# Attention on one core: a group's two softmax-sum accumulators are folded into one by an adding DMA before TensorE sums over keys

## What is computed

```python
x = x + 0.5 * ffn(layernorm(x), ...)      # 64 experts, top 6, plus a shared one
x = x + attn(layernorm(x), ...)
x = x + 0.5 * ffn(layernorm(x), ...)

def attn(x, ...):                          # 16 query heads of 32, one key/value head
    scores = einsum('bhsd,btd->bhst', q, k) / sqrt(32)
    attn = softmax(scores, axis=-1)        # over t, 2048 keys
    out = einsum('bhst,btd->bhsd', attn, v)
    return out.reshape(b, s, 512) @ Wo + bo
```

## Time and profile before

| | |
|---|---|
| median of 3 runs | 3182.35 us (3176.6 to 3187.31) |
| profiled execution | 3182.29 us |
| its span, first to last instruction | 3180.6 us |
| TensorE busy | 2770.0 us (87%) |
| VectorE | 2046.3 us (64%) |
| ScalarE | 1522.7 us (48%) |
| GpSimd | 2218.7 us (70%) |
| mean granted TensorE clock | 0.934 of full speed |
| DMA moved | 575.78 MB |

### The profile page before, as it was taken

The page is one execution under the profiler, slowest core; times in us unless marked ns, Lnnn a source line. Parts: engine busy times, 40 slices in busy tenths (PEclk is TensorE's granted clock), DMA queues, the critical chain, the costliest instruction groups (busy, mean ns, idle before and its releaser), DMA issues. The chain is left out here.

```text
span 3180.6 us, 44938 instructions
## 1 busy us (share of the span) xinstructions
PE 2770.0 (87%) x15264; PEld 1651.1 (52%) x15264; DVE 2046.3 (64%) x3922; ACT 1522.7 (48%) x2871; POOL 2218.7 (70%) x1430
## 2 busy tenths in 40 slices
PE   7967777388899999999999999999999776888870
PEld 4644444166455555555555555555554464555540
DVE  7843222267788878788787887887874394333334
ACT  5522222153466656566566665665656351222220
POOL 2248888462489879799798897997978323777770
PEclk9978888689999999999999999999999877999995
DMA  5669999895377777678676776776766364999998
GB/s 211 220 198 244 237 241 242 184 272 189 83 157 161 144 159 147 137 170 160 143 162 134 167 144 139 164 150 155 148 135 140 121 219 135 212 236 240 236 184 322
DMA packets 216987, 575.78 MB, mean 181 GB/s; under 512 B 33980, under 2 KB 35004, under 8 KB 192824
## 3 DMA queue, kind: packets, MB, share of 16 engines
q0 software_dynamic: 87296, 343.98, 53.7%
q1 hardware_dynamic: 125240, 220.55, 21.4%
q10 hardware_dynamic: 4224, 8.39, 0.7%
HBM read 230.94 MB, written 155.24 MB: 121 GB/s over the span
## 5 line engine op out<-in xcount | busy, mean ns | idle before, releaser
L1914 DVE TENSOR_REDUCE attention_mx<-attention_pM 128x1 f32<-128x512 f32 x1984 | 1209.3, 682 | 197.0 <-PE attention_pM L1797 196.3
L1744 ACT ACTIVATE attention_prob<-attention_pS 128x512 f32<-128x512 f32 x2048 | 1032.7, 624 | 592.2 <-PE attention_pS L1776 591.8
L1691 POOL TENSOR_TENSOR attention_pair<-attention_prob 128x1024 f32<-128x1024 f32 x380 | 949.6, 2504 | 210.0 <-ACT attention_prob L1744 199.3
L1776 PE MATMUL attention_pS<-attention_qT,prep_kT 128*128 128x512 f32 x2048 | 840.6, 412 | 3.1 <-ACT attention_prob L1744 2.2
L1797 PE MATMUL attention_pM<-prep_kT,attention_qT 96*128 96x512 f32 x1984 | 788.2, 398 | 1.8 <-DVE attention_mx L1914 1.1
L1776 PEld LDWEIGHTS attention_pS<-attention_qT,prep_kT 128*128 128x128 f32 x2048 | 387.5, 190 | 308.9 <-issue 210.2
L1825 PE MATMUL attention_pO<-attention_prob,attention_v 128*32 128x512 f32 x4096 | 491.7, 598 | 0.0
L768 POOL DMA_INDIRECT sum<-experts_res,c_table x256 | 403.7, 1577 | 125.4 <-issue 79.4
L1797 PEld LDWEIGHTS attention_pM<-prep_kT,attention_qT 96*128 96x128 f32 x1984 | 377.9, 190 | 92.0 <-DVE attention_mx L1914 16.5
L752 POOL DMA_INDIRECT experts_rows<-xn_rows,c_table x256 | 250.7, 979 | 103.8 <-issue 70.1
L797 PE MATMUL experts_pT<-c_ident,experts_rows 128*128 128x128 f32 x1024 | 169.8, 307 | 120.8 <-issue 46.8
(11 more groups left out here) (181 smaller groups left out, 3135.1 us busy)
## 6 DMA issues: line engine op xcount, KB each, us to landing
prep_acc<-attention_pair POOLq DMA_DIRECT2D x96, 1024.0 KB, 7.6
attention_acc<-attention_pair POOLq DMA_DIRECT2D x90, 1024.0 KB, 7.3
attention_qT<-q_parts SPq DMA_DIRECT2D x96, 256.0 KB
xn_rows<-route_xn SPq DMA_DIRECT2D x16, 1152.0 KB, 6.6
experts_wup<-in_L_ffn_w_up_dram SPq DMA_DIRECT2D x64, 256.0 KB
q_parts<-prep_acc SPq DMA_DIRECT2D x64, 256.0 KB, 4.3
ahead_wup<-in_L_ffn_w_up_dram SPq DMA_DIRECT2D x64, 256.0 KB, 9.0
combine_got<-sum SPq DMA_DIRECT2D x16, 1024.0 KB
```

What stands on the lines that cost most here:

```text
L1691: pool.tensor_tensor(to[:, part], prob[2 * n % PROBS][:, part], prob[(2 * n + 1) % PROBS][:, part], ALU.add).then_inc(s_pair, 1)
L1744: act.activation(prob[t % PROBS][:, h * QT:(h + 1) * QT], pS[:, at, :], ACT.Exp).then_inc(s_ex, 1)
L1776: pe.matmul(pS[:, n % 3, :], kT[:, key:key + P], qT[g][:, h, :], start=True, stop=True).then_inc(s_sc, 1)
L1914: dve.tensor_reduce(mx[:, unit, part:part + 1], pM[:, r % RING, :], X, ALU.max).then_inc(s_mr, 1)
```

## The change

Each group that has accumulators gets one more adding DMA, `fold`, which adds accumulator 1 onto accumulator 0. GpSimd issues it in the next group after `add_pair` 1 and before `normalise`, and waits first until all brings of that group have landed. TensorE's `denominators` then waits for the fold alone and has four matmuls, on accumulator 0, for eight. The last group is left as it was.

```diff
+        s_fold = m.sems("fold", 2)
...
+                def fold(c, g):
+
+                    for n in range(2):
+                        pool.wait_ge(s_acc[g % 2][n], (c * 2 + (g // 2 + 1)) * (3 * 16))
+                        pool.sem_inc(k["pool_on"], 1)
+                    pool.dma_start(acc[g % 2][0][:, :], acc[g % 2][1][:, :], accum_op=ALU.add
+                                   ).then_inc(s_fold[g % 2], 16)
+
...
                     for n in range(PAIRS):
                         add_pair(c, g, n)
+                        if n == 1 and G > 0:
+                            fold(*divmod(G - 1, GPC))
                         if n == 1 and G > 1:
                             normalise(*divmod(G - 2, GPC))
...
                     bank_free(r)
-                    for n in range(2):
-                        pe.wait_ge(s_acc[g % 2][n], (c * 2 + (g // 2 + 1)) * (3 * 16))
-                        for h in range(HG):
-                            ins = pe.matmul(pM[h * DH:(h + 1) * DH, r % RING, :], k["ones32"][:, :],
-                                            acc[g % 2][n][:, h * QT:(h + 1) * QT], start=n == 0, stop=n == 1)
+                    pe.wait_ge(s_fold[g % 2], (c * 2 + (g // 2 + 1)) * 16)
+                    for h in range(HG):
+                        ins = pe.matmul(pM[h * DH:(h + 1) * DH, r % RING, :], k["ones32"][:, :],
+                                        acc[g % 2][0][:, h * QT:(h + 1) * QT], start=True, stop=True)
                     ins.then_inc(s_mp, 1)
```

## The result

The change made the kernel slower. Its median is 3226.2 us (3210.9 to 3254.7, 4 runs) against 3183.4 us before (3176.6 to 3187.3, 4 runs), a ratio of 1.0147 with a 95% interval from 1.0074 to 1.022. The forecast was 3155.5 us, with a range from 3148 to 3170. The profiled execution after took 3223.04 us, its span is 3221.3 us.

A forecast was written before the change was run, and what follows sets the result against it. The prediction took TensorE's list in attention as the bound: 31 x 0.87 = 27.0 us gained, every added wait or issue costing zero, so 3155.5 us from 3182.35, with a range from 3148 to 3170.

The forecast's parts named there:

- What bounds the kernel: In attention, TensorE's list of matmuls sets the end; what is taken off it shortens the kernel.
- The price of the four matmuls: TensorE's sums: dropping accumulator 1's matmuls saves 0.87 us per group, 27.0 us over 31, between 25.4 and 29.8.
- The period of 47.8 us: Interval between the sums of neighbouring plain groups on TensorE, forecast to fall to 47.8 us from 48.7.
- The 38 us of the estimate: TensorE's sums priced by the skill page with the row's 0.598 us: 1.22 us a group; the prediction rejected it.
- The fold's landing: The fold's DMA lands in 7 to 10 us, before TensorE's sums need it: 0 us of wait.
- B: Fold late for the sums in 7 groups where SP stores and loads, by up to 1.4 us: 3162 us; chance 0.12.
- C: Fold's DMA at half a bring's pace, 13.8 us; sums stand 2.0 us in 24 groups: 3203 us; chance 0.07.
- D: No change: GpSimd eats the freed time as the period shrinks, 42.6 of 47.8 us busy: 3179 us; chance 0.06.
- GpSimd's wait: GpSimd, before the fold, waits for the group's last bring to land: 0 to 2.2 us, mostly under 1.
- ScalarE's cover: ScalarE needs pair 2's first half from GpSimd; 5.7 us of slack against at most 2.8 of wait plus issue.
- The cost of that wait: GpSimd's delay at the fold costs the kernel's end zero, since only ScalarE needs its results, with 5.7 us slack.
- The sum: All terms over the whole kernel add to -27.0 us, giving 3155.5 us.

The follow-up runs named there:

- e3: Kernel before, no fold; TensorE sums accumulator 0 alone with a matrix of twos, half the sums: 3154.7 us against 3179.3 before.
- e9: Changed kernel with the fold issued behind the normalising product and VectorE's small subtraction left out: 3146.4 us against 3177.7 before.
- e1: Changed kernel, fold in place, with VectorE's small subtraction (low part of the shifts) left out: 3155.5 us against 3179.3 before.
- e4: Changed kernel, fold waited for, but all eight matmuls of the sums put back: 3192.8 us against 3179.3 before.
- e5: Kernel before, no fold, GpSimd delayed by three fillings of an unused tile (3.6 us planned): 3241.3 us against 3181.3 before.
- e8: Kernel before, no fold, GpSimd delayed by one filling of an unused tile (1.2 us planned): 3182.2 us against 3181.3 before.
- e10: Kernel before, no fold, GpSimd delayed by two fillings of an unused tile (2.4 us planned): 3178.2 us against 3177.7 before.
- e2: Kernel before, no fold, with VectorE's small subtraction left out: 3177.0 us against 3179.3 before.
- e6: Kernel before with GpSimd delayed by three fillings of an unused tile and VectorE's small subtraction left out: 3178.7 us against 3181.3 before.

## Why the prediction was wrong

*What bounds the kernel.* Right: TensorE's list. e3 and e9 show that what is taken off it arrives. (The starts in the earlier trace rows are 0.24 and 0.31 us apart, not 0.23; and the lower end of the range adds up to 3147, not 3148. Nothing hangs on either.)

*The price of the four matmuls.* Right: 0.87 us forecast, 0.88 seen in the row, and 24.6 us for 31 groups in e3, a little under the 25.4 of my lower end; its interval reaches from 18 to 29. The period of 47.8 us is there too: in e3 the sums of the first two groups start at 906.1 and 953.9. The 38 us of the estimate by the Trainium skill, page "TensorE: Matmul & The Clock Gate", section "Measured speedup vs the span model", did not appear.

*The fold's landing.* Right: 6.9 to 10.6 us, never waited for by the sums. Rivals B and C did not happen; C had the sign and not the mechanism. D comes nearest, with waits that I didn't see, but they were not GpSimd's share of the period.

*GpSimd's wait.* Undersized. I took 0 to 2.2 us, mostly under 1; the fold's line shows 55.7 us in 29 waits, 1.9 each, and the waits between 1000 and 2400 us in e1 reach 4.2. Two things were missing. About 0.57 us pass between the landing of the last bring and the fold, which I put at nothing: in group 10 of e4 the bring was issued at 1354.30 and took 9.62 us, so 1363.92, and the fold stands at 1364.49. With the period of before, in e4, the waits at the fold are already 36.9 us in 29:

```profile
  DMA prep_acc<-attention_pair: 18.5, 14
  DMA attention_acc<-attention_pair: 18.4, 15
```

And in the changed kernel the last bring lands later, 9.4 us after its issue in the median against 8.5 before and in e4. Why is not settled; no run was made for it. ScalarE's cover was nearly right: it waited for pairs 4.0 us in all.

*The cost of that wait.* This is the step that failed: "Who needs them? ScalarE", "Cost to the end: zero. The cover is that 5.7 us". I asked only who waits for GpSimd's results by a semaphore. VectorE waits for none inside the groups, and yet it stopped, because its subtraction shared something with GpSimd's additions. The true cover was not the 5.7 us of ScalarE but the idle time up to pair 5: 0.90 us, which I had quoted, and 1.92 us, of which the change itself took 0.87. Late by 0.6 + 1.9 us on the mean, GpSimd missed it in 17 of 23 plain groups, 16 of them with a subtraction over 1 us. Misses came in rows: in groups 6 to 8 the subtraction took 4.3, 4.9 and 4.9 us, and the last brings of these groups took 10.3, 10.3 and 11.2 us to land, where e4 has 8.5, 8.3 and 8.7. What makes them late there is open; e4's one caught group had no such row behind it. e5, e8 and e10 place the threshold between 2.3 and 3.5 us, where 0.90 + 1.92 = 2.8 lies.

*The sum.* From the start of the first group's sums to the start of the last group's there are 1558.6 us before (906.9 to 2465.5), 1602.2 after (907.4 to 2509.6) and 1532.9 in e3 (906.1 to 2439.0): the change lost 69.3 us against its own TensorE half. Of that, 38.0 us are TensorE's new idle time at the maxima (39.8 - 1.8). The seven stretches above have a mean clock of 0.977, worth 0.023 x 1400 = 32 us of full speed. Together 70 us. So in the change the clock nearly doubled the price of the stops. That isn't a fixed factor: in e5 the idle time at the maxima grew by as much (36.7 us, 34.9 more than before), but the mean clock from 1000 to 2400 us was 0.99, and the time grew by 60 us. The subtraction took 64.3 us in all there, 55.2 more than before.

## What to carry to other kernels

Before making an engine later by a microsecond, look not only for who waits on its results but for operations of its neighbour that read two SBUF operands at the same time: list the small VectorE `tensor_tensor` rows, with their maximum beside their median, and see what GpSimd does at their starts. The line before the change, 189/214/2380, would have told of it. An operation that is cheap only because of the moment at which it starts has a threshold and no slope, so halves of a change that are harmless alone can be dear together. Where TensorE is full, count each stop with the slower clock that follows it.

## What was not expected of the hardware

- A 128x16 subtraction of VectorE with two SBUF inputs took 0.19 to 0.22 us when it began in the last 0.17 us of an addition of GpSimd's or met none, and up to 5.6 us (median of all 32 in the change 1.07 us) when it began earlier in one. It ended 0.04 to 0.07 us after an addition, and often not after the one that it had met: in the e5 case above 0.23 us lie between the two additions (1450.22 to 1450.45), and it ended with the second. What decides between the two is not shown. The additions grew too, the last one in the group shown from 2.69 to 3.58 us.
- A stop of TensorE of 3.1 us was followed by 6.8 us at a granted clock of 0.50 (the 1.2 GHz level). Before the change no stretch of attention between 1000 and 2400 us was under 1.00.
- Removing the subtraction without the fold brought 2.3 us (e2), and 2.6 us below before even with three fillings (e6); both are too little to be told from nothing.
